# Two decoder layers on one core: where weight splits, K evictions and turns stand in the hand-written orders of the engines

## The reference, cut to what matters

```python
x = x + L0_attn(layernorm(x))            # "gqa": 32 query heads, 8 kv heads, 16 wide; weights are sign(w) times a row scale
x = x + L0_xattn(layernorm(x), ctx)      # "xat": 32 heads of 128, rms-normed q and k
x = x + L0_ffn(layernorm(x))             # "ffn": see below
x = x + L1_attn(layernorm(x))            # "mqa": 32 query heads, one kv head, 16 wide; alibi, causal
x = x + L1_xattn(layernorm(x), ctx)      # "cga": 32 query heads, 8 kv groups, 16 wide; mask over keys
x = x + L1_ffn(layernorm(x))             # "moe": main product, 8 LoRA experts, gate of two layers, top 2
# L0_ffn, 1792 hidden units in 56 blocks of 32:
inter = xf @ c1_w.T @ c2_w.T                       # rank 16
idx = argmax(inter.reshape(-1, 56, 32), -1) + 32 * arange(56)
out = relu(dot(w1[idx], xf)) combined with w2t[idx]
```

## Time and profile before

| | |
|---|---|
| time, median of 3 runs | 2533.76 us (2530.43 to 2536.49) |
| the profiled execution, its own time | 2531.64 us |
| span of its profile | 2529.8 us |
| TensorE busy | 2341.4 us, 93% |
| weight loads (PEld, beside TensorE) | 1865.3 us |
| DVE / ScalarE / GpSimd busy | 1340.9 / 1026.9 / 650.5 us |
| granted TensorE clock, mean | 0.971 of full |

### The profile page before, as it was taken

How to read it: one execution, slowest core, us unless ns; L and a number is a source line. 1 busy time by engine, 2 the same in 40 slices (tenths; PEclk the granted TensorE clock), 3 DMA queues, 4 the chain that set the end, 5 groups by cost and what they waited for, 6 DMA issues and landing times. The chain is left out here.

```text
span 2529.8 us, 43031 instructions
## 1 busy us (share of the span) xinstructions
PE 2341.4 (93%) x17714; PEld 1865.3 (74%) x17714; DVE 1340.9 (53%) x2497; ACT 1026.9 (41%) x1749; POOL 650.5 (26%) x433
## 2 busy tenths in 40 slices
PE   6998999999999999999999799999889986999787
PEld 4676777777787877777777587787767765777576
DVE  5766534343333533343343777786645554564565
ACT  5555453445455443535444311111244443554331
...
DMA packets 22354, 80.82 MB, mean 32 GB/s; under 512 B 3360, under 2 KB 5536, under 8 KB 16032
## 3 DMA queue, kind: packets, MB, share of 16 engines
...
## 5 line engine op out<-in xcount | busy, mean ns | idle before, releaser
L2337 PE MATMUL xat_TP<-xat_Wo,xat_oT_hi 128*128 128x512 f32 x1024 | 322.5, 396 | 5.8 <-issue 5.8
L103 PE MATMUL xat_G<-xat_xnT_hi,xat_Wq 128*128 128x512 f32 x768 | 249.3, 397 | 0.0
L2337 PEld LDWEIGHTS xat_TP<-xat_Wo,xat_oT_hi 128*128 128x128 f32 x1024 | 187.3, 188 | 58.1 <-issue 22.4
L2035 POOL TENSOR_TENSOR xat_T<-xat_T,xat_mask 128x512 f32<-128x512 f32 x64 | 81.7, 1300 | 526.2 <-DVE xat_T L2117 526.2
L2337 PE MATMUL xat_TP<-xat_Wo,xat_oT_lo 128*128 128x512 f32 x512 | 199.6, 390 | 0.0
L2144 DVE TENSOR_TENSOR X<-X,xat_TP 128x512 f32<-128x512 f32 x128 | 87.0, 679 | 202.5 <-PE xat_TP L2337 202.5
L2108 DVE RECIPROCAL xat_q_inv_rms<-xat_OT 128x16 f32<-128x16 f32 x32 | 8.3, 258 | 329.0 <-PE xat_OT L2264 329.0
L103 PEld LDWEIGHTS xat_G<-xat_xnT_hi,xat_Wq 128*128 128x128 f32 x768 | 144.3, 188 | 34.2
L103 PE MATMUL ffn_H<-ffn_w,ffn_xnT_hi 128*128 128x448 f32 x512 | 147.7, 370 | 13.4 <-DVE ffn_h_kept L1203 13.2
L1113 ACT ACTIVATE ffn_hT_hi<-ffn_TP 128x384 fp32r<-128x384 f32 x64 | 34.9, 546 | 300.6 <-PE ffn_Y L1249 253.2
L103 PE MATMUL xat_G<-xat_xnT_lo,xat_Wq 128*128 128x512 f32 x384 | 151.8, 395 | 0.0
...
## 6 DMA issues: line engine op xcount, KB each, us to landing
xat_weights_raw<-in_Cq_q SPq DMA_DIRECT2D x16, 1024.0 KB, 4.8
xat_weights_raw<-in_Cq_o SPq DMA_DIRECT2D x16, 1024.0 KB, 4.8
xat_kv_raw<-in_Cq_kv SPq DMA_DIRECT2D x7, 1024.0 KB, 6.9
cga_ctxT_raw<-in_ctxT SPq DMA_DIRECT2D x4, 1024.0 KB, 5.6
out<-X SPq DMA_DIRECT2D x4, 1024.0 KB, 4.3
...
X<-in_x SPq DMA_DIRECT2D x2, 1024.0 KB, 7.0
```

Of the source, the lines that this page charges most:

```text
L103: last = eng.matmul(out, a, b, start=(n == 0), stop=(n == len(steps) - 1))
L2035: eng.tensor_tensor(T[:, n, :, :], T[:, n, :, :], mask[:, :].unsqueeze(1).to_broadcast([P, ROWS, SEQ]), ALU.add)\
L2337: last = eng.matmul(TP[m % 2][:, :], x, w, start=(n == 0), stop=(n == len(steps) - 1))
```

## The change

It has eight parts. No computation is added or removed.

1. SyncE, mqa and cga: the load of weight o is issued right behind v.
2. ScalarE: the high part of Wo (gqa: its sign and magnitude) moves from the end of slot 0 into the prologue: in mqa ahead of the K eviction, together with Wv's; in cga behind q0's eviction, together with Wv's; in gqa behind q1's.
3. GpSimd: the low part of Wo moves into the prologue, behind Wv's and ahead of shift(0).
4. ScalarE, all three: the K eviction moves behind keep_PT(2s-3).
5. cga: product q2 moves ahead of scores(0).
6. ffn: C1's high part on ScalarE moves ahead of tile 1's, the first weight split ahead of tile 2's; C1's low part moves from DVE to GpSimd, with a semaphore of its own.
7. ffn: DVE's splits 4, 6 and 8 move behind the h_kept part of their slot.
8. moe: `turn_x(i+1)` is cut in two. Tiles 0 and 1 are turned between the first two main products and split behind the first addition; tiles 2 and 3 as before.

```diff
@@ small_attention @@
+    plan = attention_plan(cross)
+        first = ["x0", "x1", "x2", "x3"] + (["q0", "q1", "k", "q2"] if cross else ["k", "q0", "q1"])
@@ SyncE @@
+            if not sign:
+                eng.dma_start(PK(ro), dram["o"]).then_inc(w_landed[3].sem, 16)
             if alibi:
...
@@ ScalarE @@
+            if alibi:
+                weight_hi("v")
+                weight_hi("o")
             for item in order[ST:len(first)]:
                 keep(item)
                 if alibi and item[1] == "k":
                     ln.scalar_sd(eng, 1)
-            if not sign:
-                weight_hi("v")
+                if cross and item[1] == "q0":
+                    weight_hi("v")
+                    weight_hi("o")
+            if sign:
+                weight_hi("o")
+                weight_abs(3)
             for s in range(LASTP + 4):
                 if 2 <= s < LASTP + 2:
                     keep_PT(2 * s - 4)
                 for item in filled(s, 0):
-                    keep(item)
+                    if item[1] != "k":
+                        keep(item)
                 if 2 <= s < LASTP + 2:
                     keep_PT(2 * s - 3)
+                for item in filled(s, 0):
+                    if item[1] == "k":
+                        keep(item)
                 for item in filled(s, 1):
                     keep(item)
...
-                if s == 0:
-                    weight_hi("o")
-                    if sign:
-                        weight_abs(3)
@@ GpSimd @@
-                for name in ("q2", "q3", "v"):
+                for name in ("q2", "q3", "v", "o"):
                     weight_lo(name)
                 for s in range(LASTP):
                     shift(2 * s)
                     shift(2 * s + 1)
-                    if s == 0:
-                        weight_lo("o")
@@ attention_plan @@
-            a[0], b[0], a[1] = [(0, "q2"), (0, "vt")], [(0, "q3")], [(0, "vp")]
+            a[0] = [(0, "vt")] if cross else [(0, "q2"), (0, "vt")]
+            b[0], a[1] = [(0, "q3")], [(0, "vp")]
@@ sparse_ffn, ScalarE @@
             ln.scalar_first_sd(eng, 2)
+            eng.wait_ge(c_landed[0].sem, c_landed[0].at(0, 16))
+            eng.activation(C1[0][:, :, :], c1room, ACT.Copy).then_inc(c_hi.sem, 1)
             ln.scalar_hi(eng, 0, 1, I[1])
             ln.scalar_first_sd(eng, 3)
-            eng.wait_ge(c_landed[0].sem, c_landed[0].at(0, 16))
-            eng.activation(C1[0][:, :, :], c1room, ACT.Copy).then_inc(c_hi.sem, 1)
+            high(0)
             ln.scalar_hi(eng, 0, 2, I[0])
-            high(0)
@@ sparse_ffn, GpSimd (removed from DVE) @@
+            eng.wait_ge(c_hi.sem, c_hi.at(0, 1))
+            eng.tensor_tensor(C1[1][:, :, :], c1room, C1[0][:, :, :].bitcast(F32), ALU.subtract)\
+               .then_inc(c1_lo.sem, 1)
@@ sparse_ffn, DVE, vector_pass @@
-                    if not fresh:
-                        for n in LOW_BY_VECTOR.get(s, ()):
-                            low(eng, n)
                     u = s - 1
                     if 0 <= u < NU:
...
+                    if not fresh:
+                        for n in LOW_BY_VECTOR.get(s, ()):
+                            low(eng, n)
@@ lora_experts, DVE @@
-                half = mains[i][:2]
-                for w in half:
-                    add_main(w)
+                add_main(mains[i][0])
+                if i + 1 < NST:
+                    low(i + 1, (0, 1))
+                add_main(mains[i][1])
                 gate_scale(i)
                 if i + 1 < NST:
-                    low(i + 1)
+                    low(i + 1, (2, 3))
@@ lora_experts, TensorE @@
-                for w in mains[i][:2]:
-                    main_product(w)
+                main_product(mains[i][0])
                 if i + 1 < NST:
-                    turn_x(i + 1)
+                    turn_x(i + 1, (0, 1))
+                main_product(mains[i][1])
+                if i + 1 < NST:
+                    turn_x(i + 1, (2, 3))
```

More of the change, by code:

```diff
@@ L235, in small_attention @@
     W1 = HD + 1
-    plan = attention_plan()
+    plan = attention_plan(cross)
     with ExitStack() as ctx:
@@ L339, in small_attention @@
         PIECE = {name: n for n, name in enumerate(piece_order)}
-        first = ["x0", "x1", "x2", "x3"] + (["q0", "q1", "k"] if cross else ["k", "q0", "q1"])
+        first = ["x0", "x1", "x2", "x3"] + (["q0", "q1", "k", "q2"] if cross else ["k", "q0", "q1"])
         order = [(0, name) for name in first]
@@ L932, in _, with attention_plan @@
                     make(item)
-def attention_plan():
+def attention_plan(cross):
     n = 2 * ST
@@ L1491, in normed, with low @@
                     ln.vector_xn(eng, i, t)
-            def low(i):
+            def low(i, tiles):
                 ln.off = i * STOK
-                for t in range(ST):
+                for t in tiles:
                     ln.vector_lo(eng, i, t, TURN[t % 2])
@@ L1636, in weights_ready, with turn_x @@
                 eng.wait_ge(w_lo.sem, w_lo.at(0, n + 1))
-            def turn_x(i):
-                for t in range(ST):
+            def turn_x(i, tiles):
+                for t in tiles:
                     if t >= 2:
@@ L2492 @@
     "c_landed_0",
+    "c_lo_by_pool",
     "c_landed_1",
```

16 lines of the change are left out of this document (7 added, 9 removed).

## The result

| | before | after |
|---|---|---|
| median of 6 runs each | 2532.9 us (2530.43 to 2537.97) | 2486.77 us (2483.0 to 2489.2) |
| span of the profiled execution | 2529.8 us | 2485.5 us |
| TensorE busy | 2341.4 us | 2333.7 us |

The ratio of the times is 0.9814, 95% interval [0.9801, 0.9827]. The forecast was 2488, from a sum of 45.9 us gained on the profiled execution. The medians are 46.1 us apart; the spans of the two profiled executions, which the sum is to be held against, 44.3.

The account below looks back on a forecast made before the run. TensorE, busy 2341.4 us (93% of the span), was taken as the bound, with savings only in its waits and half clock. Six terms summed to 45.9 us: 2531.64 to 2485.7, about 2488 as a median; range 2475 to 2505.

Parts of the forecast that it names:

- mqa, 7 us: Alibi attention's start: moving Wo's split removes up to 6.2 us of stall before turn(1), plus 1.5 us of clock; bounds 4.5 to 7.7.
- cga, 11.4 us: Cross attention's start: 7.2 us from Wo's earlier split, 4.2 from q2 filling the wait of scores(0); bounds 8 and 12.
- most of 1.7 us of slow clock: Cross attention behind scores(0): with q2 filling the 2.60 us wait, TensorE also regains most of this half-clock time.
- gqa, 4.5 us: Bitnet attention's start: the 2.95 us wait for Vbd goes, plus 1.5 us of clock; bounds 2 and 5.2.
- K eviction, 13.3 us: Three small attentions: with PT ahead of the K eviction, nine waits of 1.48 us go; bounds 8 and 15.
- Feed-forward, 5 us: Feed-forward start: C1's low part on GpSimd and later DVE splits make h_kept some 5 us earlier; bounds 1 and 7.5.
- C1's low part meets DVE's LayerNorm scalings: Feed-forward start: two scalings lie under GpSimd's 1.3 us split, costing 0.9 us, inside the lower bound.
- Expert stage, 4.7 us: Turns' waits for xnT_lo: first gone (1.96 us), second about 1.1 (saves 1.7), third shorter by 1.0; bounds 2 and 7.
- Rival (a): Expert stage: with a shorter wait the clock may not fall, giving 7 to 8 us more, 2480 us; chance 25%.
- (b): Stalls return elsewhere: K's bank, late feed-forward splits, q1's eviction in cga, half the expert gain; 2502 us; chance 18%.
- (c): Slower: the K eviction behind PT holds the next product and scores(2s); 2542 us at 6 us each; chance 1%.
- (d): Little effect: something beside GpSimd's split held PT, stalls stay under other names; within 5 us of 2534; chance 2%.

Follow-up runs that it names:

- experiment 2: Changed kernel with Wo's load, high part and low part put back behind slot 0, q2 in cga still ahead of scores(0): 2502.99 us (ratio 0.9889).
- experiment 3: Changed kernel with cga's product q2 put back behind scores(0): 2486.76 us (ratio 0.9821).
- experiment 8: Changed kernel with ScalarE's whole feed-forward order as before, C1's low part staying on GpSimd: 2485.32 us (ratio 0.9805).
- Experiment 9: Changed kernel with the expert stage's main products spread 4, 3, 3, 6 over the groups in place of 4, 4, 2, 6: 2484.04 us (ratio 0.9794).

## Why the prediction was right, point by point

- **What bounds the kernel.** Right: the 44.3 us came out of TensorE's waits (36.6) and its half clock (7.7), on the same matmuls.
- **mqa, 7 us:** 6.24 in the traces, 6.1 by experiment 2. The waits went as counted (6.18 to 1.79, and 1.02 for Vbd to none): turn(1) comes 5.56 us earlier, foretold 5.6. I had 1.5 us for the clock's end, and got 0.7.
- **cga, 11.4 us:** 9.89. Wo's part is 6.7 (foretold 7.2), q2's 2.65 to the turn(1) in place of 4.2. The step that failed is "most of 1.7 us of slow clock": the clock behind scores(0) did stay up, and fell behind the next wait instead. By its gain in time q2's move is unresolved, and in experiment 3 the clock stayed up behind scores(0) even with the 2.60 us wait back.
- **gqa, 4.5 us:** 3.9 in the traces (8.48 less 4.54 for its K evictions), with 2 us of clock play on either side in ten kernels. At equal granted clock it is 2.7 (experiment 2): the wait is confirmed, the 1.5 us of clock added to it is not.
- **K eviction, 13.3 us:** 14.5. The bank was not waited for. The bracket of 1.48 was taken as the whole cost; it is 1.65 at the spot and 1.6 on average over the path.
- **Feed-forward, 5 us:** 2.36, the one term that was wrong by half. The prediction put 0.9 us on "C1's low part meets DVE's LayerNorm scalings", from a mean over four scalings, and it looked at one GpSimd split alone. Two things were missed: a held scaling waits for the whole remainder of the split, not for a share of its own length, and the high part that part 6 moves on ScalarE starts a second, longer split under the fourth scaling. Together 2.5 us (0.77 + 1.73) on the chain that sets the first product. The trace of before had what was needed: the fourth scaling ended at 1405.7 us, and GpSimd's first weight split, which followed ScalarE's high part, began at 1407.7, so a high part moved one place ahead could bring the split under it. In the other half, H(2), the mechanism was right: experiment 8, where no split holds a scaling, has H(2) and H(4) 4.7 us earlier than before, and of these 1.5 go back to the clock.
- **Expert stage, 4.7 us:** 4.79; the waits foretold as 0, 1.1 and about 2 were 0, 1.01 and 1.01 with 2.68 for the gate's turn. The third turn saved 0.75 us where 1.0 was counted, the second 1.86 for 1.7.
- **Rival (a), the clock stays up in the expert stage:** it fell. Experiment 9 took the wait away and the clock fell elsewhere. **(b)** came near in one of its four parts, the feed-forward (2.36 us where it said 1 and the forecast 5), for another reason than late splits. **(c) and (d)** have nothing for them: TensorE has no wait for Kbd in the changed kernel, and where 6.18 us stood, 1.79 is left, for the same producer.
- **The sum** was good also by luck: 5.5 us too much for feed-forward (2.6), cga (1.5), mqa (0.8) and gqa (0.6), against 1.2 too little for K, 1.6 of half clock that went from behind mqa's first K eviction, and 1.0 net in stretches that were not foretold at all.
